# Chunk 0's first k pairs from k itself, and a new order of the first steps, in a token-mixing and expert block

## The reference

```
t = _ln_c(x) as tokens                       # layer norm over channels
q, k = l2norm(silu(t @ Wq)), l2norm(silu(t @ Wk));  v = silu(t @ Wv)
beta = sigmoid(t @ Wb)
# per head:  u_t = beta_t * (v_t - S_{t-1}^T k_t)
#            S_t = S_{t-1} + k_t u_t^T
#            o_t = S_t^T q_t
x = x + t + o @ Wo
```

## Time and profile before

| what | value |
|---|---|
| runs, median of 3 | 486.1 us (484.05 to 486.39) |
| profiled execution, span from first to last instruction | 484.3 us |
| busy: PE, VectorE, ScalarE, GpSimd | 416.3, 416.6, 352.6, 412.6 us |
| instructions | 10459 |
| DMA | 42.91 MB, 89 GB/s |

### The profile page before, as it was taken

One profiled execution on the slowest core, in us unless ns is written; L12 is line 12 of the kernel. 1 busy time (PEld: TensorE's weight loads), 2 busy tenths in 40 slices (PEclk: granted clock), 3 DMA queues, 4 the chain that ended last, 5 costly groups with the idle time before them and its releaser, 6 DMA issues.

```text
span 484.3 us, 10459 instructions
## 1 busy us (share of the span) xinstructions
PE 416.3 (86%) x2400; PEld 383.9 (79%) x2400; DVE 416.6 (86%) x2290; ACT 352.6 (73%) x1035; POOL 412.6 (85%) x527
## 2 busy tenths in 40 slices
PE   1445265899999999999999999999999989999996
PEld 0323144798898999999999989898989889899895
DVE  4259889999999999999999999999999999996200
ACT  3699366587878787787869696969696847485862
POOL 5478698999999999999999999999999999986340
PEclk9999999999999999999999999999999999999999
DMA  6568383633242323223232323322332232300301
GB/s 165 162 131 169 92 163 90 146 93 111 50 118 70 97 65 91 72 89 84 70 84 87 91 83 83 92 81 71 92 102 69 74 99 73 98 3 1 115 1 16
DMA packets 43437, 42.91 MB, mean 89 GB/s; under 512 B 20144, under 2 KB 35184, under 8 KB 43376
## 3 DMA queue, kind: packets, MB, share of 16 engines
q1 hardware_dynamic: 42768, 42.05, 33.2%
q10 hardware_dynamic: 608, 0.21, 0.2%
HBM read 35.95 MB, written 6.29 MB: 87 GB/s over the span
## 4 chain that ended last, share of the span: by engine, by line
DVE 41%; PE 24%; POOL 10%; issue 8%; ACT 8%; SPq 6%; DMA 3%; POOLq 0%; ACTq 0%; DVEq 0%
DVE Pr L1378 9%; DVE bank L1382 9%; DVE u L1380 8%; DVE SH L1386 7%; PE bank L454 5%; POOL PQ L932 3%; POOL PQ L925 3%; ACT L733 3%; PE bank L427 2%; PE bank L439 2%; PE bank L431 2%; PE bank L429 2%; PE bank L430 2%; PE bank L428 2%; POOL hid L970 2%
## 5 line engine op out<-in xcount | busy, mean ns | idle before, releaser
L970 POOL TENSOR_TENSOR hid<-sg,ug 128x192 f32<-128x192 f32 x192 | 112.9, 607 | 22.4 <-ACT ug L699 19.0
L925 POOL TENSOR_TENSOR PQ<-SH,QB 128x768 f32<-128x768 f32 x62 | 112.8, 1841 | 0.4 <-DVE SH L1386 0.4
L932 POOL TENSOR_TENSOR PQ<-PQ 128x768 f32<-128x768 f32 (+2 forms) x93 | 103.0, 1107 | 6.1
L454 PE MATMUL bank<-Wd,hidT 128*128 128x192 f32 x576 | 106.6, 326 | 0.0
L698 ACT ACTIVATE sg<-bank 128x192 f32<-128x192 f32 x192 | 63.6, 331 | 58.3 <-PE bank L431 48.3
L1382 DVE TENSOR_TENSOR bank<-bank,u 128x96 f32<-128x96 f32 (+1 forms) x467 | 104.2, 264 | 0.1
L1378 DVE TENSOR_TENSOR Pr<-SH,bank 128x96 f32<-128x96 f32 (+1 forms) x437 | 100.8, 265 | 3.5 <-PE bank L394 1.3
L1380 DVE TENSOR_REDUCE u<-Pr 128x6 f32<-128x102 f32 (+1 forms) x437 | 102.3, 268 | 0.6 <-issue 0.2
L1386 DVE TENSOR_TENSOR SH<-SH,bank 128x96 f32<-128x96 f32 (+1 forms) x467 | 101.7, 254 | 0.3
L454 PEld LDWEIGHTS bank<-Wd,hidT 128*128 128x128 f32 x576 | 94.5, 190 | 0.0
L427 PE MATMUL bank<-Whi,hiT 128*128 128x384 f32 (+1 forms) x192 | 73.6, 383 | 1.3 <-DVE loT L1134 1.1
(11 more groups left out here) (147 smaller groups left out, 817.0 us busy)
## 6 DMA issues: line engine op xcount, KB each, us to landing
QB<-q_scratch SPq DMA_DIRECT2D x64, 384.0 KB
k_scratch<-khl SPq DMA_DIRECT2D x64, 48.0 KB, 1.7
KR<-k_scratch SPq DMA_DIRECT2D x32, 96.0 KB, 2.4
q_scratch<-qn SPq DMA_DIRECT2D x64, 24.0 KB, 1.6
Wd<-in_L_ffn_w_down_dram SPq DMA_DIRECT2D x4, 288.0 KB, 8.9
out_dram<-xT SPq DMA_DIRECT2D x1, 896.0 KB, 4.1
Wlo_unsplit<-in_L_ffn_w_gate_dram SPq DMA_DIRECT2D x2, 384.0 KB, 4.5
Wlo_unsplit<-in_L_ffn_w_up_dram SPq DMA_DIRECT2D x2, 384.0 KB, 5.4
```

Source lines behind the costliest of these rows:

```text
L454: last = mm(bDn[:, 0:C], hidT[:, turn_half(g), k - lo, :], Wd[:, k, :], start=False, stop=(k == KT - 1))
L925: tt(PQ[:, at * BR * HP:(at + n) * BR * HP].rearrange("p (i b h) d -> p i b (h d)", i=n, b=BR), SH[:, lo:lo + n].rearrange("p i b h d -> p ...
L932: chained(tt(PQ[:, :, 0:w], PQ[:, :, 0:w], PQ[:, :, w:2 * w], ALU.add))
L970: tt(hid[:, r * H:(r + 1) * H], sg[:, m % RING], ug[:, m % RING], ALU.mult).then_inc(s_hid, 1)
```

## The change

1. `Direct`: 32 selector blocks made from the identity, 16 copies on VectorE before the first step, after one memset on GpSimd. `fill_direct` uses them to spread the first two pairs of chunk 0 from kn itself, 8 fp32 products a pair; pairs 2 to 7 still come from KR.
2. PE, steps -2 to 0: the fills of chunk 0 move between the stages of tiles 1 to 3.
3. VectorE: step -1 has only `A_vT(0)`; tile 1's work and tile 2's statistics stand in slots 3 to 29 of chunk 0, tile 2's work and tile 3's statistics in slots 42 to 61.
4. ScalarE: both halves of `place(0)` move to step -2, `A_khi(1)` into step -1, the first half of `place(1)` stands in step 0.
5. GpSimd: separate orders for steps -3 to 0. The clearing of the spare buffers goes behind `rsqrt` of step -3; in step 0 `rsqrt` stands behind `reading(0)`, two weight parts, `summing(0)` and one more part.
6. SP: the load of x for tiles 4 to 15 goes from step -1 into step 0, between `scratch_q(1)` and `spread_q(1)`.

```diff
 EARLY = 14
+DIRECT = 2
 FIRST = 4
...
     Sel = sb("Sel", [P, T // 2, BP, HX, D], F32R)
+    Direct = sb("Direct", [P, DIRECT, BR, 2, HX, BP, HX, D])
     QB = sb("QB", [P, BR, T, HP, D])
...
     s_sel, s_fill = sem("selectors_ready"), sem("KB_pair_filled")
+    s_dzero, s_direct = sem("direct_selectors_cleared"), sem("direct_selectors_ready")
     s_pair, s_pq, s_oT = sem("state_pair_ready"), sem("states_read"), sem("o_summed")
...
           at(1, scratch_q)
+          once(c, 0, load_later)
           at(1, spread_q)
-        if c == -1:
-          load_later()
         for i in range(KT // 3):
...
-        if f == 0:
+        if f == (DIRECT if c == 0 else 0):
           if c == 0:
...
+      def fill_direct(f):
...
+        if f == 0:
+          pe.wait_ge(s_direct, DIRECT * BR * 2 * HX)
+          pe.wait_ge(s_kf, 1)
+        for r in range(BR):
+          for j in range(2):
+            at = (r * 2 + j) * G
+            for x in range(HX):
+              last = mm(bKB[f % 2][:, at:at + G], Direct[:, f, r, j, x].rearrange("p b x e -> p (b x e)"), kn[:, x, :],
+                   start=(x == 0), stop=(x == HX - 1))
+        last.then_inc(s_fill, 1)
...
         at = partial(stage, c, par)
-        if c < 1:
-          at(0, fill, 3)
+        if c == -2:
           at(3, A_x)
-          at(0, fill, 4)
-          at(0, fill, 5)
-          at(0, fill, 6)
+          fill_direct(0)
+          at(3, A_h)
+          fill_direct(1)
+          at(3, A_vb)
+          at(2, fill, 2)
+          at(3, A_qk)
+        elif c == -1:
+          at(3, A_x)
+          at(1, fill, 3)
+          at(3, A_h)
+          at(1, fill, 4)
+          at(1, fill, 5)
+          at(3, A_vb)
+          at(1, fill, 6)
+          at(3, A_qk)
+        elif c < 1:
+          at(3, A_x)
           at(0, fill, 7)
           at(1, fill, 0)
+          at(3, A_h)
           at(1, fill, 1)
-          at(3, A_h)
           at(1, fill, 2)
...
         if c < 1:
-          if c >= 0:
-            at(1, A_khi)
           at(3, A_xs)
...
           once(c, 0, weights_hi1, 4)
-          at(0, place, 1)
+          once(c, 0, place, 1, 1, 0)
           if 0 <= c + 2 < NC:
...
           at(3, A_plus)
-          at(1, place, 0)
           once(c, 0, weights_hi1, 5)
...
           at(3, A_xh)
+          once(c, -2, place, 0, 0, 0)
+          once(c, -2, place, 0, 0, 1)
+          once(c, -1, A_khi, 1, 1)
           once(c, -1, weights_hi0, 8)
...
           pool.wait_ge(s_khi, a)
+        if a == 1:
+          pool.wait_ge(s_fill, DIRECT)
         chained(tt(ksc[:, :, :], inv[:, 12:24].rearrange("p (x h) -> p x h", x=HX),
...
+      def clear():
...
+        for b in free:
+          pool.memset(b, 0.0).then_inc(s_clear, 1)
...
         at = partial(stage, c, par)
-        if c < 1:
-          once(c, -1, weights_lo0, 3)
-          once(c, 0, weights_1, 4)
-          if c <= NC:
-            rsqrt(c)
+        if c == -3:
+          rsqrt(c)
+          clear()
+        elif c == -2:
+          rsqrt(c)
+          at(2, A_kn)
+          at(2, A_vn)
+          at(2, A_klo)
+          at(2, A_qn)
+          weights_lo0(0)
+          weights_lo0(1)
+          weights_lo0(2)
+        elif c == -1:
+          weights_lo0(3)
+          rsqrt(c)
+          weights_lo0(4)
+          at(2, A_vn)
+          at(2, A_kn)
+          weights_lo0(5)
+          weights_lo0(6)
+          at(2, A_klo)
+          at(2, A_qn)
+          weights_lo0(7)
+          weights_lo0(8)
+          weights_1(0)
+          weights_1(1)
+          weights_lo0(9)
+          weights_lo0(10)
+          weights_lo0(11)
+        elif c == 0:
           at(0, reading, 0)
-          once(c, -1, weights_lo0, 4)
-          once(c, -2, A_kn, 0, 0)
-          at(2, A_vn)
-          once(c, 0, weights_1, 5)
-          if c > -2:
-            at(2, A_kn)
-          once(c, -2, A_klo, 0, 0)
-          once(c, -1, weights_lo0, 5)
-          once(c, -1, weights_lo0, 6)
-          once(c, -1, weights_lo0, 7)
-          once(c, -1, weights_lo0, 8)
-          once(c, -1, weights_1, 0)
-          once(c, -1, weights_1, 1)
+          weights_1(2)
+          weights_1(3)
           at(0, summing, 0)
-          at(2, A_qn)
+          weights_1(4)
+          rsqrt(c)
           at(0, reading, 1)
           at(0, summing, 1)
-          once(c, -2, weights_lo0, 0)
-          once(c, -1, weights_1, 2)
-          once(c, 0, weights_1, 6)
-          once(c, -1, weights_lo0, 9)
-          if c > -2:
-            at(2, A_klo)
-          once(c, 0, weights_1, 7)
-          once(c, -1, weights_lo0, 10)
-          once(c, -1, weights_1, 3)
-          once(c, -2, weights_lo0, 1)
-          once(c, -2, weights_lo0, 2)
-          once(c, 0, weights_lo0, 11)
+          weights_1(5)
+          at(2, A_vn)
+          at(2, A_kn)
+          weights_1(6)
+          at(2, A_qn)
+          at(2, A_klo)
+          weights_1(7)
         elif c < NC:
...
       pool.memset(SH[:, T - 1], 0.0).then_inc(s_zero, 1)
+      pool.memset(Direct[:, :, :, :, :, :, :, :].rearrange("p f r j x b y e -> p (f r j x b y e)"), 0.0).then_inc(s_dzero, 1)
       pool.memset(Wpz[:, :], 0.0).then_inc(s_wpz, 1)
-      for b in free:
-        pool.memset(b, 0.0).then_inc(s_clear, 1)
+      pool.memset(hlo[:, :].bitcast(F32), 0.0).then_inc(s_low0, 1)
       pool.memset(loT[:, :, :].bitcast(F32), 0.0).then_inc(s_low0, 1)
-      pool.memset(hlo[:, :].bitcast(F32), 0.0).then_inc(s_low0, 1)
       pool.wait_ge(s_const, 4)
...
-          if c < 1:
-            at(-1, 1, A_vT)
+          if c < -1:
             at(11, 2, A_low)
...
             at(48, 3, A_bias)
+          elif c == -1:
+            at(-1, 1, A_vT)
+          elif c == 0:
+            at(3, 1, A_low)
+            at(4, 1, A_low_tail)
+            at(14, 1, A_z)
+            at(20, 2, A_stats)
+            at(22, 2, A_mean)
+            at(23, 2, A_var)
+            at(26, 1, A_ss)
+            at(29, 2, A_bias)
+            at(37, 1, A_vT)
+            at(42, 2, A_low)
+            at(43, 2, A_low_tail)
+            at(51, 2, A_z)
+            at(52, 3, A_stats)
+            at(54, 3, A_mean)
+            at(56, 3, A_var)
+            at(59, 2, A_ss)
+            at(61, 3, A_bias)
           elif c < NC:
...
          rows[:, :, 1, :, i].unsqueeze(3).to_broadcast([P, BP, HX, D]), ALU.add).then_inc(s_sel, 1)
+      dve.wait_ge(s_dzero, 1)
+      token = ident[:, :].rearrange("p (b r t) -> p b r t", b=BP, r=BR)
+      for f in range(DIRECT):
+        for r in range(BR):
+          for j in range(2):
+            for x in range(HX):
+              nc.vector.tensor_copy(Direct[:, f, r, j, x, :, x], token[:, :, r, 2 * f + j].unsqueeze(2)
+                         .to_broadcast([P, BP, D])).then_inc(s_direct, 1)
       chunks(step)
```

## The result

The changed kernel takes 493.03 us (median of 4 runs, 492.38 to 493.87), the kernel before in the same runs 485.63 us (484.05 to 486.39): ratio 1.0151, 95% interval 1.0123 to 1.0178. It is **7.4 us slower**, 1.5%; forecast were +4.0 us. The profiled executions have spans of 491.5 and 484.3 us.

The account below looks back on a forecast made before the run. The recurrence on VectorE bounds from 84 us; in the first 57 us no engine is full. Starting 7.3 us earlier, but delayed through GpSimd's queue, the mark comes 4.0 us later: 486.1 us becomes 490.1 us, range 484.5 to 495.0 us.

Parts of the forecast that it names:

- The failed step: GpSimd before the first step: clearing and reordered memsets fall into its idle time before 16.8 us, counted as hidden.
- the mark: Start of the statistics of tile 0's y on VectorE, chunk 1; forecast 74.3 against 70.37 us, 4.0 us later.
- the `Direct` copies: Sixteen new VectorE copies before the first step: 2.2 us in all, hidden with 0.8 us to spare.
- first product: Start of the recurrence on VectorE in chunk 0: at 23.6 instead of 30.96 us, 7.3 us earlier.
- rs of tile 2: GpSimd's `rsqrt` for tile 2, during chunk 0: begins at 33.6 instead of 27.69 us, 5.9 us later.
- rs of tile 3 done: End of GpSimd's `rsqrt` for tile 3, behind a 23.5 us queue and 0.4 us of waits: 57.5 us.
- kn done: GpSimd's kn of tile 2, awaited by ScalarE's step 1: at 67.1 us instead of 50.64 us.
- VectorE's stand in slot 61: Late in chunk 0, VectorE waits 5 us for GpSimd's `rsqrt` of tile 3; chunk 1 begins at 58.4 us.
- The 72.5 us for VectorE's order alone: Time of the mark if only VectorE's order counted; the chain through GpSimd was said to end last.
- The direct products: PE's `fill_direct` in chunk 0: 16 matmuls at 0.215 us, 3.45 us a pair, first ready at 23.6 us.
- rival 3: Weight loads of PE's direct fills not hidden: 7.8 us a pair, 498.9 us, or 494.5 us half hidden; chance 0.13.
- Rival 1: Recurrence keeps its early start if VectorE never stands in slot 61: 3.6 us won, 482.5 us; chance 0.17.

Follow-up runs that it names:

- a1_clear: Changed kernel, with GpSimd's nine memsets of the spare buffers begun only after the projection weights are split; 490.38 us, ratio 1.0100.
- a2_rs: On a1_clear, GpSimd's `rsqrt` of tile 3 right behind the first `reading` of chunk 0; 489.89 us, ratio 1.0084.
- a3_kn: On a1_clear, GpSimd's vn and kn of tile 2 right behind `rsqrt`, ahead of the second `reading` and `summing`; 488.80 us, ratio 1.0063.
- a6_order: On a1_clear, GpSimd's step 0 reordered: vn, kn, qn of tile 2 ahead of the second `reading`, six `W1` parts last; 485.45 us, ratio 1.0000.
- a10_order: On a6_order, `rsqrt` of step 1 before two weight parts, tile 2's statistics and bias and tile 1's sums of squares earlier, GpSimd reordered; 483.33 us, ratio 0.9963.
- a7_order: As a6_order, with seven more GpSimd weight parts behind the first `reading` and the first `summing` ahead of `rsqrt`; 488.11 us, ratio 1.0056.

## Why the prediction was right in sign and short in size

**The failed step** is one clause: "`clear` and the reordered memsets fall into GpSimd's idle time before 16.8 us". GpSimd was idle; VectorE was not, and its copy stood in the memsets' way. I checked the cover on the engine that does the work and not what runs beside it. The term was put at nothing and measures 2.9 us on the copy, 2.75 us on the first projection (15.14 us against 12.40 us) and 2.5 us at the mark when it is taken out (a1_clear). Of the 3.4 us by which the forecast was short, the mark has 3.0 us (6.93 us measured, 3.93 us by the prediction's figures), nearly all of it this term; the other 0.4 us lie behind the mark and around the span, and are no more than the runs spread. The Trainium skill, "SBUF — State Buffer", section "Who interferes with whom", says that a copy or cast of VectorE in its two-port mode and a GpSimd instruction take a shared pair of ports as an exclusive lock, and that the one that comes second blocks fully. The trace agrees that it blocks (3.40 and 0.46 us), but the block lasts for a row of nine memsets, longer than the one instruction of which the Trainium skill speaks there; which mode the copy ran in, no run shows. I had used this rule in the prediction for the `Direct` copies, where three memsets run, and left its price out of the sum. It was paid there too:

```profile
L1471 DVE COPY Direct<-ident x16: 175/181/1208, 4.2 to 6.6; 128x64 f32<-128x64 f32 x16
```

The three figures are the shortest, the median and the longest of the sixteen copies in ns. The first, begun at 4.16 us, ends at 5.37 us, just behind the last of the three memsets (5.31 us); from then on one comes every 0.10 us. So 2.59 us against 2.2 us is near by luck: a copy costs less than the 0.14 us that were taken, and some 0.9 us of holding make up for it. They stayed hidden with 0.7 us to spare. The second pair of instructions of the same kind, 5 us later, I had not looked for.

**Without that term the sum holds.** +4.0 us was forecast; a1_clear, which has all the rest of the change, has its mark 4.43 us behind the earlier trace rows (0.2 us of it a later start of that execution) and its time 4.6 us above the kernel before. Step by step, with 2.75 us added to each forecast for the changed kernel: first product 26.35 us (measured 26.39), rs of tile 2 36.35 us (35.43), rs of tile 3 done 60.25 us (59.55), chunk 1 61.15 us (60.44), kn done 69.85 us (70.14), mark 77.05 us (77.30). VectorE's stand in slot 61 was put at 5 us and is 5.26 us, that of slot 32 at 2.4 us and is 2.56 us. Two small misses cancel, which is luck: rs of tile 2 came 0.9 us earlier than the forecast with the 2.75 us added, and the second `reading` stood 0.98 us for VectorE, which itself had waited for rs; the sum had no such wait. One reading was wrong without harm: the prediction puts the profiled execution (484.3 us) at the low end of the runs, but that is a span, and the other runs of the kernel before have 1.9 to 2.0 us between span and time, so it stands near their upper end. The 72.5 us for VectorE's order alone are given there without a sum.

**The direct products** went as the row said: 16 matmuls in 3.70 us (3.45 us forecast) with their weight loads beside them, 3.49 us in the same stretch. That disposes of rival 3; the trace doesn't agree with the rule of the Trainium skill, "TensorE: Matmul & The Clock Gate", "Part 3: Packing small matmuls — row/col tiling", as I had applied it there.

**Rival 1 had the wrong condition.** It was to decide when VectorE never stands in slot 61. In a2_rs it never does, and 489.89 us is far from 482.5 us. By a2_rs, a3_kn and a6_order it is when GpSimd gets through kn, qn and the two readings that decides. a10_order has the last `summing` done at 61.78 us and takes 483.33 us, near the rival's figure. That alone isn't enough either: a7_order has it done at 61.90 us and takes 488.11 us, because the weight parts left over delay the next rs.

**Not settled.** What the direct start is worth once GpSimd's order is right, as said above; and why rs of tile 2 is 0.9 us early. Part of it can be the second direct pair, which took 2.88 us, so that VectorE did not stand the 0.8 us that the prediction has there.

## What to carry over

When a piece of work moves into another engine's idle time, look at who runs beside it there, not only at whether the engine is free. When one engine (here GpSimd, some 33 us from rs of tile 2 to the last `oT` in the changed kernel) has the longest queue, an earlier start elsewhere can turn into waiting: in a1_clear the recurrence starts some 7 us earlier and the mark comes 4.4 us later. What helped was the order of that queue, the useful results first and the parts that nobody reads yet last, as far as they delay nothing behind. A wait that disappears tells nothing by itself: a2_rs removed 5 us of VectorE's standing for 0.75 us at the mark, a6_order won 6.65 us at the mark by a new order of one step, of which the medians keep 4.9 us.

## What the runs showed of the hardware

A float32 to float32r copy of 128x588 on VectorE takes 0.46 us alone, 1.24 us beside three GpSimd memsets and 3.40 and 3.41 us beside nine; beside memsets it ends 0.31 or 0.32 us after the last one each time, so it doesn't get in between two of them. A `Direct` copy of 128x64, one of which comes every 0.10 us when alone, took 1.21 us beside three.

TensorE rose to its upper level (2.4 GHz) in chunk 0 of the changed kernel. Timeline of PE there, and busy time by stretch, where the granted clock is the third figure from the end (1.00 is the upper level, 0.50 the lower, 1.2 GHz):

```profile
30.27 0.34 PE L365 MATMUL bank<-Wphi,hhi 128*128 128x384 f32 x1
...
30.79 0.34 PE L368 MATMUL bank<-Wphi,hlo 128*128 128x384 f32 x1
```

```profile
22.00:28.00 6.00, 5.35 (x25) 5.34 (x26) 1.99 (x11) 3.84 (x13) 4.01 (x6) 0.50 0.14 33
29.00:35.00 6.00, 3.18 (x19) 2.30 (x17) 6.00 (x38) 4.35 (x9) 1.77 (x2) 1.00 0.55 133
53.00:93.00 40.00, 18.55 (x53) 13.63 (x54) 29.61 (x167) 24.70 (x62) 33.40 (x39) 0.50 0.51 125
```

Products of 384 columns come every 0.17 to 0.18 us at the upper level and every 0.32 us at the lower (47.52 to 48.80 us). The rise is at 28.6 us, in the second direct pair; ahead of it PE had worked almost without a gap from 22.65 us on. The fall is at 35.4 us; ahead of it PE had had nothing to do since 33.4 us. From 49.0 to 52.4 us the clock is at the upper level once more, then at the lower until 93 us. In the kernel before the granted clock is printed as 1.00 throughout, but the pace is 0.32 us until 86.3 us, in chunk 2, and 0.18 us behind it: there the level has to be read from the pace. What the rise in chunk 0 was worth at the mark no run shows.
